# Loading the scan block's input and first weights inside the block before, and storing the rates with one DMA

## What is computed

```python
def layer0(x):                                   # x: 4 x 512 x 512
    xn = layernorm(x)
    return x + ttt(xn) + ffn(xn)

def ttt(h):                                      # 32 heads of 16, chunks of 16 tokens
    XQ, XK, XV = h @ q_w.T, h @ k_w.T, h @ v_w.T
    eta = token_idx * sigmoid(h @ lr_w + lr_b) / 16          # the rates
    for each chunk:                              # W1, b1 are the carried state
        Z1 = xk @ W1 + b1
        grad = backward of a layernorm at Z1 against xv - xk
        Z1_bar = xq @ W1 - (eta * tril(xq @ xk.T)) @ grad + b1 - tril(eta) @ grad
        W1 = W1 - (last_eta * xk).T @ grad
        b1 = b1 - sum(last_eta * grad)
        out = xq + layernorm(Z1_bar)
    return post_norm(out) @ o_w.T

def ffn(h):
    g, u = (h @ gate_w.T) * gate_s, (h @ up_w.T) * up_s      # 1408 wide
    return ((silu(g) * u) @ down_w.T) * down_s
```

## Time and profile before

| | us |
|---|---|
| median of three runs | 2056.87 |
| lowest and highest | 2054.27, 2058.54 |
| the profiled execution | 2057.76 |
| its span in the trace | 2055.8 |
| PE busy | 1897.7 |
| border between the two blocks, SP passes | 194.1 |
| first FFN matmul | 204.16 |

### The profile page before, as it was taken

The page is one execution under the profiler, slowest core; times in us unless marked ns, Lnnn a source line. Parts: engine busy times, 40 slices in busy tenths (PEclk is TensorE's granted clock), DMA queues, the critical chain, the costliest instruction groups (busy, mean ns, idle before and its releaser), DMA issues. The chain is left out here.

```text
span 2055.8 us, 34803 instructions
## 1 busy us (share of the span) xinstructions
PE 1897.7 (92%) x12632; PEld 1432.0 (70%) x12632; DVE 1199.4 (58%) x2368; ACT 1003.7 (49%) x2169; POOL 1026.5 (50%) x904
## 2 busy tenths in 40 slices
PE   5897998898998999798899989999999999999998
PEld 3676776666666665487677766777777777777776
DVE  4662565686876764355334446666666666666653
ACT  3332555565565655466433325444444444444442
POOL 5453566566655654420133317655555555555552
PEclk9998999999999999989999999999999999999999
DMA  7776647335434432131578772122233223322321
GB/s 247 281 284 211 202 152 267 106 116 208 119 114 155 164 110 97 52 125 67 200 239 258 240 264 82 60 113 92 83 131 117 87 84 131 115 83 83 113 96 48
DMA packets 157111, 297.97 MB, mean 145 GB/s; under 512 B 20240, under 2 KB 97296, under 8 KB 150288
## 3 DMA queue, kind: packets, MB, share of 16 engines
q1 hardware_dynamic: 155856, 294.70, 42.4%
q10 hardware_dynamic: 1088, 1.05, 0.2%
HBM read 221.52 MB, written 74.19 MB: 144 GB/s over the span
## 5 line engine op out<-in xcount | busy, mean ns | idle before, releaser
L1975 POOL TENSOR_SCALAR probs<-probs,rsum 128x512 f32<-128x512 f32 x256 | 396.1, 1565 | 245.6 <-DVE rsum L2111 245.6
L2075 ACT ACTIVATE p_tok<-bank 128x512 fp32r<-128x512 f32 x256 | 154.5, 607 | 344.1 <-PE bank L2015 344.0
L2107 DVE TENSOR_REDUCE nmax<-bank 128x1 f32<-128x512 f32 x256 | 158.9, 682 | 95.5 <-PE bank L2007 95.5
L2117 DVE TENSOR_TENSOR p_tok<-bank,p_tok 128x512 fp32r<-128x512 f32 x256 | 173.2, 679 | 15.8 <-ACT p_tok L2075 15.8
L2067 ACT ACTIVATE probs<-bank,nmax 128x512 f32<-128x512 f32 x256 | 172.8, 692 | 3.6 <-DVE nmax L2107 3.6
L1456 POOL TENSOR_TENSOR y_pieces<-y_tok,y_pieces 128x512 fp32r<-128x512 f32 x48 | 61.4, 1296 | 210.3 <-ACT y_pieces L1670 210.3
L60 PE MATMUL bank<-xs,ffn_w 128*128 128x512 f32 x352 | 152.6, 434 | 12.2 <-issue 8.4
L2015 PE MATMUL bank<-ident,probs 128*128 128x128 f32 x1024 | 155.7, 276 | 2.8 <-DVE p_tok L2117 2.8
L2015 PEld LDWEIGHTS bank<-ident,probs 128*128 128x128 f32 x1024 | 121.5, 140 | 50.8 <-issue 27.2
L1090 DVE SCALAR_TENSOR_TENSOR pt<-bank,t_mask 128x256 f32<-128x256 f32 x256 | 91.7, 413 | 98.0 <-PE bank L877 96.7
L61 PE MATMUL bank<-xs,ffn_w 128*128 128x512 f32 x352 | 138.7, 394 | 0.0
(11 more groups left out here) (279 smaller groups left out, 4980.0 us busy)
## 6 DMA issues: line engine op xcount, KB each, us to landing
ffn_w<-ffn_pieces SPq DMA_DIRECT2D x120, 512.0 KB, 3.6
uvo<-uvo_pieces SPq DMA_DIRECT2D x15, 2048.0 KB, 8.4
wq<-wq_pieces SPq DMA_DIRECT2D x16, 1536.0 KB, 6.3
ffn_pieces<-stage SPq DMA_DIRECT2D x30, 512.0 KB, 4.1
xs<-xn_pieces SPq DMA_DIRECT2D x4, 2048.0 KB, 8.1
y_tok<-in_gup SPq DMA_DIRECT2D x32, 256.0 KB, 3.1
wk<-wk_pieces SPq DMA_DIRECT2D x16, 512.0 KB, 3.6
ffn_w<-ffn_pieces SPq DMA_DIRECT2D x16, 384.0 KB, 3.5
```

The costliest lines, as they stand in the source:

```text
L1975: nc.gpsimd.tensor_scalar(probs[:, u % 8, :], probs[:, u % 8, :], rsum[:, u % 8:u % 8 + 1], None, ALU.mult).then_inc(norm_done, 1)
L2075: nc.scalar.activation(p_tok[:, Q % 2, 0, :, hh * P:(hh + 1) * P], banks[4 + u % 2][:].rearrange("p (k q) -> p k q", k=NBLK), ACT.Copy).th ...
L2107: nc.vector.tensor_reduce(nmax[:, u % 8:u % 8 + 1], banks[u % HG][:], axis=X_AXIS, op=ALU.max, negate=True).then_inc(max_done, 1)
L2117: nc.vector.tensor_tensor(p_tok[:, Q % 2, 1, :, q], banks[4 + u % 2][:].rearrange("p (k q) -> p k q", k=NBLK), p_tok[:, Q % 2, 0, :, q].bi ...
```

## The change

Five edits:

1. `xs` and `ffn_w` get fixed addresses at the start of the first block's region. The order of the weights there is changed: key weights first (hi and lo, 16 KB of each partition), then the values', then the queries'. `xs` takes the place of the key weights, the first four of the five slots of `ffn_w` that of the value weights, the fifth lies in the query weights. The second block allocates a placeholder over both.
2. At `t` = 3, after the stores of pieces 28 to 30 (slot 0), SP waits until the keys' products are done, and loads `xs` from the first token block's stored input.
3. In `move_rates`, after the rates' store, SP waits until the values' products are done, and for the store of each piece, and loads weight pieces 0 to 3 (`NEARLY`).
4. The rates are stored in one DMA of 256 KB instead of four of 64 KB. The eight loads are as before.
5. The second block's opening no longer loads `xs` and pieces 0 to 3: `cst` of step 0 comes first, then piece 4, `cst` of step 1 and `acc`. The semaphores `xs_in` and `fw_in` are made ahead of both blocks.

```diff
@@ -135,11 +135,15 @@
         ff_sc = s0("ffn_scales", [P, 2, NI])
         hd = lambda ap: ap.rearrange("p (x d) -> p x d", d=HD)
         over_d = lambda ap: ap.unsqueeze(2).broadcast_to([P, NX, HD])
+        NWP, NEARLY = 5, 4
+        xs_in, fw_in = sem("ttt_xs_in"), [sem(f"ttt_fw_in{i}") for i in range(NWP)]
 
         with ExitStack() as st:
             s = sb_in(st)
-            kw_h, qw_h, vw_h = [s(n + "_hi", [P, NF, HID], F32R) for n in ("kw", "qw", "kvw")]
-            kw_l, qw_l, vw_l = [s(n + "_lo", [P, NF, HID], F32R) for n in ("kw", "qw", "kvw")]
+            first_home = (nc.sbuf_base + 31) // 32 * 32
+            kw_h, kw_l, vw_h, vw_l, qw_h, qw_l = [s(n, [P, NF, HID], F32R) for n in ("kw_hi", "kw_lo", "kvw_hi", "kvw_lo", "qw_hi", "qw_lo")]
+            xs = nc.alloc_sbuf_tensor_at("xs", [P, 2, NF, TB], F32R, offset=first_home)
+            fw = nc.alloc_sbuf_tensor_at("ffn_w", [P, NWP, 2, NF, P], F32R, offset=first_home + 16 * 1024)
             x_sb, xc = s("x_sb", [P, NF, TB]), s("xc", [P, NF, TB])
             xs_hi, xs_lo = s("xs_hi", [P, NF, TB], F32R), s("xs_lo", [P, NF, TB], F32R)
             sq, x_sum, v_sum, std = s("sq", [P, 2, TB]), s("x_sum", [P, TB]), s("v_sum", [P, TB]), s("std", [P, TB])
@@ -250,9 +254,13 @@
 
                     def move_rates():
                         sp.wait_ge(sig_done, 2)
-                        for b in range(BATCH):
-                            sp.dma_start(lr_dram[b].rearrange("(m n) t e x -> (n t) m (e x)", m=NF), lr_raw[:, NF * b:NF * b + NF, :]).then_inc(lr_out, 16)
-                        sp.wait_ge(lr_out, 16 * BATCH)
+                        sp.dma_start(lr_dram.rearrange("b (m n) t e x -> (n t) (b m) (e x)", m=NF), lr_raw[:]).then_inc(lr_out, 16)
+                        sp.wait_ge(job_ready, JT * (NTB - 1) + 2 * NF)
+                        for w in range(NEARLY):
+                            sp.wait_ge(st_out[w % NST], 16 * (w // NST + 1))
+                            n = width(JOBS_T[w])
+                            sp.dma_start(fw[:, w, :, 0:n, :].bitcast(F32), fw_pc[w][:, :, 0:n, :]).then_inc(fw_in[w], 16)
+                        sp.wait_ge(lr_out, 16)
                         for b in range(BATCH):
                             for e in range(2):
                                 c = 32 * b + 16 * e
@@ -267,6 +275,10 @@
                                 store_piece(i)
                                 for r in raw_of[i]:
                                     load_raw(r + NRAW)
+                            if slot == 0 and t == NTB - 1:
+                                sp.wait_ge(job_ready, JT * t + NF)
+                                sp.wait_ge(xs_out, 32)
+                                sp.dma_start(xs[:].bitcast(F32), xs_pc[0]).then_inc(xs_in, 16)
                             if slot == 1 and t + 2 < NTB:
                                 load_x(t + 2)
                         if t < NTB - 1:
@@ -557,9 +569,8 @@
 
         with ExitStack() as st:
             s = sb_in(st)
-            NWP, LAG = 5, 9
-            xs = s("xs", [P, 2, NF, TB], F32R)
-            fw = s("ffn_w", [P, NWP, 2, NF, P], F32R)
+            LAG = 9
+            s("home_of_xs_and_fw", [P, 36 * 256])
             hid_hi, hid_lo = s("hid_hi", [P, 4, TB], F32R), s("hid_lo", [P, 4, TB], F32R)
             silu_g, up_sb, hid, dn_sb = [s(n, [P, 2, TB]) for n in ("silu_g", "up_sb", "hid", "down_sb")]
             acc = s("ff_acc", [P, NF, TB])
@@ -589,15 +600,14 @@
             names = ("w_done z_ready sq_done var_done std_done sg_done sgbd_dve sgbd_act ssum_done d_done wx_dve wx_act snap_done sz_done wsx_done "
                      "kz_done kt_ready kt_done qbd_done gbd_done p_ready pt_done o_done base_done ocopy_done osq_done ovar_ready ostd_done orec_done "
                      "oxh_done oy_done oq_done chain zero_done f_ready ev_gate ev_up ev_down prod_done hhi_done hlo_done acc_done "
-                     "grad_in xs_in acc_in acc_out")
+                     "grad_in acc_in acc_out")
             (w_done, z_ready, sq_done, var_done, std_done, sg_done, sgbd_dve, sgbd_act, ssum_done, d_done, wx_dve, wx_act, snap_done, sz_done, wsx_done,
              kz_done, kt_ready, kt_done, qbd_done, gbd_done, p_ready, pt_done, o_done, base_done, ocopy_done, osq_done, ovar_ready, ostd_done, orec_done,
              oxh_done, oy_done, oq_done, own, zero_done, f_ready, ev_gate, ev_up, ev_down, prod_done, hhi_done, hlo_done, acc_done,
-             grad_in, xs_in, acc_in, acc_out) = [sem("ttt_" + x) for x in names.split()]
+             grad_in, acc_in, acc_out) = [sem("ttt_" + x) for x in names.split()]
             wx_zero = sem("ttt_wx_zero")
             cst_in = [sem("ttt_cst_in0"), sem("ttt_cst_in1")]
             grad_out = [sem("ttt_grad_out0"), sem("ttt_grad_out1")]
-            fw_in = [sem(f"ttt_fw_in{i}") for i in range(NWP)]
 
             NPART = NSUPER * NF * BATCH
             NGR = NSUPER * NF
@@ -653,10 +663,8 @@
                             sp.wait_ge(acc_out, 16 * NF * t)
                         sp.dma_start(acc[:], fm(A["xT"])[:, :, t * TB:(t + 1) * TB]).then_inc(acc_in, 16)
 
-                    load_xs(0)
-                    load_fw(0)
                     load_cst(0)
-                    for j in range(1, NWP):
+                    for j in range(NEARLY, NWP):
                         load_fw(j)
                     load_cst(1)
                     load_acc(0)
```

## The result

The changed kernel takes 2064.22 us in the median of six runs (2061.11 to 2065.29), the kernel before 2056.45 beside it (2054.27 to 2060.06). The ratio is 1.0034, with a 95% interval of 1.0021 to 1.0047: it is slower, by 4.3 to 9.7 us. The forecast was 2058.8, "same", and the time lies above its range. The profiled execution took 2065.29, with a span of 2063.2; PE's own work is as large as before, so the time was lost standing still.

A forecast was written before the change was run, and what follows sets the result against it. PE's standing still was taken to bound it: the border set by SP's last DMA, then a 3.62 us weight wait. Summing -3.6 (wait), +5.5 (border) and 0 (clock) gave +1.9 on 2056.87, so 2058.8 us; range 2052.8 to 2062.2.

The forecast's parts named there:

- PE goes from `z_product(0)` straight to the first gate: -3.62 us: Behind the border between the blocks: PE's wait for the first feed-forward weights disappears, gaining 3.62 us.
- PE still comes last in step 0: First state update: PE arrives after DVE and ACT, with 2.4 us to spare, so the 3.62 us are kept.
- The border moves from 194.1 to 199.6, +5.5 us: Border between the blocks: SP passes 5.5 us later, as the rate loads queue behind the early loads.
- the walk: SP's queue from piece 30's store to the border: transfer times added in order, from 177.6 to 199.6.
- 402 GB/s: DMA engines ahead of the border: rate assumed for bulk transfers, giving 5.2 us each for `xs` and four weight pieces.
- its upper bound: Border: bulk at 312 GB/s adds 3.0 us and a slower rate store 2.5, together +11.0 instead of +5.5.
- the rates' store ... 1.9: SP's queue ahead of the border: the rates' 2048 packets take 1.9 us of engine time, to 190.9.
- ACT's eight stores ... 3.3: ACT's queue ahead of the border: the stores of `cst_stage`, sharing the engines, take 3.3 us, to 189.0.
- the queue and not the issue ends last: Last step before the border: queued transfers end at 199.6, while issue alone would have the last rate load at 198.8.
- I take 0: PE's clock at the first feed-forward matmuls: the half-speed phase is paid again, change 0, range -0.5 to +1.
- PE idles at least as long ahead of the same work: Ahead of the feed-forward matmuls: PE's unchanged or longer idling makes it pay the half-speed clock again, change 0.
- (c): Rival at the waits on `lr_out` and `lr_in`: rates' packets slow among bulk, border past 201.8, up to +7.4, 2064; chance 0.13.

The follow-up runs named there:

- e10: Changed kernel with `xs` loaded ahead of piece 28's store and the four weight pieces loaded behind the border again: 2053.58 us, ratio 0.9986 to the kernel before.
- e12: Like e3, but ACT's eight constant stores issued some 25 us earlier, leaving out the last token block's constants: 2055.37 us, ratio 1.0001 to the kernel before.
- e7: Like e10, with the eight rate loads also behind the border, between weight pieces 2 and 3, and DVE waiting for them: 2053.16 us, ratio 0.9985.
- e5: Changed kernel with the four early weight loads issued behind the eight rate loads, still ahead of the border: 2059.59 us, ratio 1.0017 to the kernel before.
- e3: Changed kernel with only `xs` loaded early, the four weight pieces loaded behind the border again: 2058.33 us, ratio 1.0020 to the kernel before.
- e1: Changed kernel with the rates stored in four DMAs again, all else as changed: 2064.06 us, ratio 1.0045 to the kernel before.
- e4: Changed kernel with only the four weight pieces loaded early, `xs` loaded behind the border again: 2059.02 us, ratio 1.0024 to the kernel before.
- e14: Like e7, with `cst_scratch` laid out so each constant store's destination is 128 rows of 256: 2050.79 us, ratio 0.9973 to the kernel before.
- e9: Changed kernel with ACT's eight constant stores issued some 25 us earlier, leaving out the last token block's constants: 2059.74 us, ratio 1.0023 to the kernel before.

## Why the prediction was wrong

Point by point, as it put them. Its times are in the frame of the trace of before; in the trace of after PE ends its query products 0.9 us later, which is added here.

- **"PE goes from `z_product(0)` straight to the first gate: -3.62 us": right.** Border to gate is 6.4 us instead of 10.1, as the text said. DVE's wait for `cst` has gone, and PE still comes last in step 0:

```profile
213.85 0.43 DVE L1116 TENSOR_TENSOR gx_gt_xh<-gx_gt_xh,cst 128x256 f32<-128x256 f32 x1
...
222.09 0.42 DVE L1085 TENSOR_TENSOR w_state<-w_state,bank 128x256 f32<-128x256 f32 x1 [2.85 <-PE bank L857]
```

  DVE waits 2.85 us for PE's update (the text's count leaves 4.7; most of the difference is that PE came 1.3 sooner), and ACT ends its half of the spread at 219.07, 2.3 ahead of it, where 2.4 was expected.
- **"The border moves from 194.1 to 199.6, +5.5 us": wrong, +9.7.** The direction, the mechanism (one queue in order, the rates paying for what stands ahead) and the place (the two waits on `lr_out` and `lr_in`) held. The terms of the walk did not:

| step of the walk | predicted, +0.9 | measured | late by |
|---|---|---|---|
| `xs` landed | 184.3 | 188.1 | 3.8 |
| rates' store landed | 192.4 | 195.7 | 3.3 |
| last weight piece landed | 197.6 | 201.9 | 4.3 |
| SP passes | 200.5 | 204.7 | 4.2 |

  (Predicted landings are the walk's last packets with its 0.6 us added. The last piece's own landing, in us from its issue at 194.1:)

```profile
DMA to landing us min/median/max: 7.8/7.8/7.8
```

  The step that failed is thus the walk from `xs` to the rates' store: 3.3 of the 4.2 us are there when the store has landed. (`xs` itself lands 3.8 late, which is more, because a landing is that of a transfer's last packet; packets of the stores behind it run from 185 on.)
- **The first mis-sized term is the rate of the bulk.** 402 GB/s had been read from a stretch of loads in packets under 8 KB. The windows (us, busy of PE, PEld, DVE, ACT, POOL, PEclk, DMA share, GB/s), and the packets from 180 to 185:

```profile
174.00:182.00 8.00, 8.00 (x37) 6.64 (x36) 2.57 (x4) 1.58 (x3) 5.92 (x7) 1.00 0.92 309
182.00:188.00 6.00, 6.00 (x29) 4.95 (x28) 1.38 (x2) 0.00 (x0) 4.58 (x4) 1.00 0.96 344
188.00:195.00 7.00, 3.32 (x15) 2.43 (x13) 1.38 (x2) 0.00 (x0) 0.00 (x0) 1.00 0.83 248
```
```profile
DMA packets 101, 1.55 MB, mean 310 GB/s; under 512 B 2, under 2 KB 7, under 8 KB 7
```

  The engines are nearly as full as foreseen (0.92 and 0.96), yet move 309 and 344 GB/s. Stores mixed in are not the reason: from 180 to 185 all but 7 packets are of 8 KB or more, as only `xs` has them (16 KB to a partition), and they move 310. At that rate `xs` takes 6.8 us instead of 5.2. It is the rate of `xs` at the border before, 312, which the prediction had worked out and kept for its upper bound. In e10's idle stretch, from 171 to 174, the same load moved 426 GB/s; why it is slower here is open.
- **The second is "the rates' store ... 1.9" with "ACT's eight stores ... 3.3".** Both were shares of the engines' time, added as if the two queues could be packed end to end. Together they hold the queues from about 188 to 195, 7 us instead of 5.2, and from 190 to 194 a third of the engines' time is idle; without ACT's stores beside them the rates' packets are through in some 2.5 us (e12). ACT's stores alone fill only 54% of the engines' time (e7), and the reading is that the rates' packets take turns with them there while the other engines have run dry; the records don't name the engine, so this is argued. The experiments show what ACT's stores cost where they stand, 4.1 to 4.3 us of border, for which the walk had 3.3.
- **The last step, "the queue and not the issue ends last", came out the other way round.** The weights took 6.2 us from the rates' store's landing to the last piece's, instead of 5.2, and from there to SP it was 2.8 (2.9 in the walk). But one issue of the eight loads was held for 2.95 us, so that the eighth went out at 202.1; it landed 2.5 later, the shortest time of the eight. So here the issue ended last. With the weights behind the loads (e5) the step from the store's landing to the border was 2.6 us shorter.
- **The clock, "I take 0": outside its range of -0.5 to +1, by chance in the change's favour.** Gate to update is 1.3 us shorter. PE's matmuls come at full pace from 212.11, 1.0 us after the first gate; before it was 4.0. PE had worked without a gap since 208.18 here, and since 204.16 before, where the wait stood just ahead of it. But that the wait is gone doesn't fix the gain: e5 has no wait either, PE works without a gap from 204.62 and passes the gate at 207.53, and the clock comes back 3.0 us behind that. The windows in which it rises, after and e5:

```profile
212.00:213.00 1.00, 1.00 (x5) 0.76 (x5) 0.59 (x3) 0.68 (x2) 1.00 (x2) 0.90 0.21 82
210.00:211.00 1.00, 1.00 (x5) 0.82 (x4) 0.93 (x3) 0.34 (x1) 0.00 (x0) 0.71 0.66 252
```

  Gate to update takes 9.9 us in e3 and 11.1 in e5, against 11.6 before. The argument "PE idles at least as long ahead of the same work" looked at the idle time alone and gives no size for this.
- **The rival that came true is (c), slower.** Its place, its cause and its border's threshold (201.8) are what the trace shows, and its price for the border with both upper bounds was near: +9.7 where the bound was +11.0. Both of its causes came about: `xs` moved at 310 GB/s where 312 was the bound, and the rates' store with ACT's took 1.8 us more than its share where the bound was 2.5. The text had the chance at 0.13 and does not say why so low. That its 2064 is the measured time is in part luck: its border was 1.3 too late, the clock's 1.3 was not in it, and the measured time has over 2 us more than the stretch shows. The rule of the Trainium skill that spoke for issuing early would have ended at a gain. The runs bear the limit that the prediction set beside it: it holds for `xs` in the empty stretch (e10) and for the weights behind the rates (e5), not ahead of a transfer that a barrier waits for.

**Open.** In eleven of the thirteen changed kernels the measured difference from before lies above that of the first update's distance (by 1.8 us in the median, 4.4 at the most; +7.0 against +4.7 in the kernel of the change). The intervals are 2 to 3 us to either side, and no place in the traces accounts for it. All thirteen are held against one trace of before, so what that trace has of its own is in every one; beyond that it may be noise or a small cost outside this stretch. It matters for the forecast: with the stretch's +4.7 alone the time would be 2061.6, inside the range, though 2.8 above the forecast. The shortfall that the traces explain is the border's, +9.7 for +5.5; the rest of the way out of the range is not explained.

## What to carry to other kernels

A load issued early is paid by whatever stands behind it in the queue; ask first who waits for that, and put bulk either in a stretch in which the queue is empty or behind the last small transfer that a barrier needs. Busy shares of two queues don't add up to a time: look at how many engines each can use, and at how many packets a microsecond come through while both are at work. And when a transfer has been seen at two rates, count with that of the stretch most like its new place, or carry both through to the chances: here the slower one, kept for a bound, was the one that came.

## What the hardware showed that was not expected

- **An issue can block the sequencer.** One DMA issue held SP for 10.1 us, with the rates' 2048 packets, three stores and `xs` still queued ahead of it (3.8 us in e1, 3.9 in e4's rate loads, 5.3 in e14's, and 6.7 in e9, where ACT's stores are not in the way); elsewhere the same issue takes 0.43. How much must be queued for this was not measured.
- **Small packets slow down beside another queue's.** 250 a microsecond beside ACT's 1 KB packets at 160, against 965 a microsecond for q1 alone in e12. The Trainium skill, "DMA: Bandwidth & Descriptors", section "Queues, rings and completion order", says that an engine takes turns between queues a whole packet at a time, of some 9 to 17 descriptors; the trace agrees in so far as both queues move in the same stretch, at 1.6 records of q1 for each of q10; how many go in one turn no run here shows.
- **The shape of a store's destination sets how many engines serve it.** 8 x 16 x 256 ran at 189 packets a microsecond and 54% of the engines' time, 128 x 256 at 367 and 99%, with equal bytes. The same page of the Trainium skill, section "Why a DMA increments its semaphore by 16 and not by 1", says that a transfer uses the largest number of engines up to 16 that divides the slowest dimension of both sides, which gives 8 and 16 here; the trace agrees.
